# Local attention: preparation moved two units earlier, and each score issued one unit ahead

## What is computed

```python
h = shift_token(x)                       # the upper 64 channels come from the token before
q, k, v = split(h @ wqkv)                # 8 heads of 64 each
q = l2norm(q) * qs
k = l2norm(k) * ksc
q, k = rotary_xpos(q, k)                 # q * cos * scale + rotate_half(q) * sin * scale, k with 1 / scale
sim = einsum('bhwid,bhwjd->bhwij', 8.0 * q, look_around(k))
sim = where((i < j) | (i > j + WINDOW) | (j == -1), -max, sim)
o = einsum('bhwij,bhwjd->bhwid', softmax(sim), look_around(v))
x = x + o @ wo
```

## Time and profile before

| | us |
|---|---|
| median of 3 runs | 8063.11 (8062.08 to 8072.71) |
| the profiled execution | 8073.38 |
| its span, first to last instruction | 8071.7 |
| mean granted clock of TensorE | 0.813 |

### The profile page before, as it was taken

The page is one execution under the profiler, slowest core; times in us unless marked ns, Lnnn a source line. Parts: engine busy times, 40 slices in busy tenths (PEclk is TensorE's granted clock), DMA queues, the critical chain, the costliest instruction groups (busy, mean ns, idle before and its releaser), DMA issues. The chain is left out here.

```text
span 8071.7 us, 121471 instructions
## 1 busy us (share of the span) xinstructions
PE 5969.8 (74%) x45848; PEld 2884.3 (36%) x45848; DVE 4107.3 (51%) x6441; ACT 2971.3 (37%) x6472; POOL 1953.7 (24%) x1781
## 2 busy tenths in 40 slices
PE   5557567786768876666678999877777798678677
PEld 3445151114442222222234544434344333344343
DVE  4333435662427745888844444344444566444444
ACT  1002323553334541444311222345355355354453
POOL 0113032212142201444511000034143011341341
PEclk6558676887888888787785887889899888899888
DMA  1001012211121100000003221111111000110110
GB/s 44 4 30 51 14 62 68 65 49 64 48 62 43 37 16 14 0 0 0 0 7 64 52 52 44 26 41 38 31 40 38 9 1 1 47 40 15 51 39 23
DMA packets 261161, 268.98 MB, mean 33 GB/s; under 512 B 113600, under 2 KB 190656, under 8 KB 258688
## 3 DMA queue, kind: packets, MB, share of 16 engines
q1 hardware_dynamic: 250368, 240.26, 11.5%
q0 software_dynamic: 10240, 21.25, 0.8%
HBM read 122.59 MB, written 71.66 MB: 24 GB/s over the span
## 5 line engine op out<-in xcount | busy, mean ns | idle before, releaser
L2170 PE MATMUL ps<-s_l2b_hc,ident 128*128 128x512 f32 x512 | 361.4, 846 | 332.6 <-DVE s_l2b_hc L2333 332.6
L1942 DVE TENSOR_REDUCE s_l3l_negmax<-ps 128x4 f32<-128x512 f32 x256 | 175.0, 683 | 744.0 <-PE ps L1783 744.0
L2118 POOL TENSOR_TENSOR s_l2b_Bx<-s_l2b_du,s_l2b_B 128x512 f32<-128x512 f32 x256 | 406.5, 1610 | 473.3 <-ACT s_l2b_B L2240 410.4
L1873 ACT ACTIVATE s_l3l_probs<-ps,s_l3l_biases,s_l3l_q_inverse 128x128 f32<-128x128 f32 x1024 | 455.6, 462 | 55.7 <-DVE s_l3l_biases L1944 55.3
L2325 DVE TENSOR_TENSOR_SCAN s_l2b_state<-s_l2b_decay,s_l2b_Bx 128x512 f32<-128x512 f32 x256 | 389.9, 1562 | 154.6 <-ACT s_l2b_decay L2246 113.3
L1721 POOL TENSOR_TENSOR s_l3l_probs<-s_l3l_probs,s_l3l_inverse 128x512 f32<-128x512 f32 x256 | 266.9, 1043 | 830.5 <-DVE s_l3l_inverse L1923 830.3
L1745 PE MATMUL ps<-s_l3l_hs,s_l3l_wqk 128*128 128x512 f32 x512 | 305.0, 703 | 177.3 <-DVE s_l3l_prod L1897 95.5
L1057 DVE TENSOR_REDUCE s_L3a_negmax<-ps 128x1 f32<-128x128 f32 (+3 forms) x512 | 236.1, 488 | 362.0 <-PE ps L893 359.5
L638 DVE TENSOR_REDUCE s_L1a_negmax<-ps 128x1 f32<-128x512 f32 x512 | 316.5, 681 | 153.3 <-PE ps L501 152.6
L1035 ACT ACTIVATE s_L3a_pt<-ps 128x256 f32<-128x256 f32 (+3 forms) x512 | 195.3, 434 | 530.3 <-PE ps L893 528.5
L908 PE MATMUL ps<-ks,s_L3a_qs 40*128 40x256 f32 (+3 forms) x1024 | 360.2, 610 | 30.1 <-DVE s_L3a_kvsq L1072 16.5
(11 more groups left out here) (658 smaller groups left out, 13547.7 us busy)
## 6 DMA issues: line engine op xcount, KB each, us to landing
s_l3l_qk<-s_l3l_rope SPq DMA_DIRECT2D x1024, 64.0 KB
scratch_rope<-s_L3a_rope SPq DMA_DIRECT2D x32, 512.0 KB, 2.8
ks<-scratch_parts SPq DMA_DIRECT2D x384, 32.0 KB
s_L3a_qs<-scratch_rope SPq DMA_DIRECT2D x64, 128.0 KB
ks<-scratch_rope SPq DMA_DIRECT2D x64, 128.0 KB
s_L0e_slots<-scratch_sent SPq DMA_DIRECT2D x16, 396.0 KB, 5.9
s_L1e_slots<-scratch_sent SPq DMA_DIRECT2D x16, 396.0 KB, 6.3
scratch_square<-s_L1a_rows SPq DMA_DIRECT2D x24, 256.0 KB, 3.0
```

What stands on the lines that cost most here:

```text
L1873: act.activation(t["probs"][:, U % (LAG + 1), k, :], ps[:, U % 2, P * k:P * (k + 1)], ACT.Exp, bias=t["biases"][:, U % (LAG + 1), k:k + 1] ...
L2118: pool.tensor_tensor(t["Bx"][:, n % 2, k, :], t["du"][:, b % 2, k, :], t["B"][:, n % 2, :], ALU.mult).then_inc(s["bx_ready"], 1)
L2170: pe.matmul(ps[:, 4 + k, :], g["ident"][:, :], t["hc"][:, n % 2, k, :], start=(n == 0), stop=(n == STATES - 1)).then_inc(s["summed"], 1)
```

## The change

TensorE's list in a unit becomes `turns(U - 2)`, `values(U - 3)`, the output in unit 3, `scores(U + 1)`, side work. Ahead of the loop stands `scores(0)`. Preparation moves by `EARLY = 2` units: in units 0 to 5 stands what stood in units 2 to 7, and units 6 and 7 hold the first two pairs of projections of batch b+2. The lists of all engines follow (`beside` in place of `prep`). What has no unit in front of it (all of batch 0, the first two pairs of batch 1) goes into `FIRST`, ahead of the loop. The semaphore of the transfers is split into one for q's 16 and one for k's 16; a rotation waits for its own half alone. `shift` moves from unit 4 to unit 3, `shift_values` stays behind unit 7, and the four values change places.

```diff
+    EARLY = 2
+
     def prep(b, u):
-        if b == BATCH:
+        if not 0 <= b < BATCH:
             return []
         if u < 4:
             return [("proj", b, u, ab) for ab in range(2)]
         if u == 4:
-            return [("norm", b), ("v", b, 1)]
+            return [("norm", b), ("v", b, 3)]
         if u == 5:
-            return [("v", b, 0), ("v", b, 3)]
+            return [("v", b, 0), ("v", b, 1)]
...
+    def beside(b, u):
+        u += EARLY
+        return prep(b + 1 + u // UNITS, u % UNITS)
+
+    FIRST = [item for u in range(UNITS) for item in prep(0, u)] + [item for u in range(EARLY) for item in prep(1, u)]
...
-        STACKED = 16 * 32
+        STACKED = 16 * 16
...
-                sp.wait_ge(s["stacked"], START + b * STACKED)
+                sp.wait_ge(s["q_stacked"], START + b * STACKED)
+                sp.wait_ge(s["k_stacked"], START + b * STACKED)
...
-                pool.wait_ge(s["stacked"], START + b * STACKED)
+                pool.wait_ge(s["q_stacked" if e < 2 else "k_stacked"], START + b * STACKED)
...
             shift(1)
+            for e in range(EARLY):
+                rotate(1, e)
             shift_values(0)
...
-                    if u < 4 and b + 1 < BATCH:
-                        rotate(b + 1, u)
-                    if u == 4 and b + 2 < BATCH:
+                    for ahead, e in ((b + 1, u + EARLY), (b + 2, u + EARLY - UNITS)):
+                        if 0 <= e < 4 and ahead < BATCH:
+                            rotate(ahead, e)
+                    if u == 3 and b + 2 < BATCH:
                         shift(b + 2)
...
-            for u in range(UNITS):
-                for item in prep(0, u):
-                    side(item)
+            for item in FIRST:
+                side(item)
+            scores(0)
             for U in range(BATCH * UNITS + BEHIND):
                 b, u = divmod(U, UNITS)
-                if b < BATCH:
-                    scores(U)
                 if LAG <= U < BATCH * UNITS + LAG:
                     turns(U - LAG)
                 if U >= BEHIND:
                     values(U - BEHIND)
                 if b and b < BATCH and u == BEHIND:
                     side(("out", b - 1))
+                if U + 1 < BATCH * UNITS:
+                    scores(U + 1)
                 if b < BATCH:
-                    for item in prep(b + 1, u):
+                    for item in beside(b, u):
                         side(item)
```

More of the change, by code:

```diff
@@ L1612, in prep @@
         return [("qinv", b), ("v", b, 2)]
+    def beside(b, u):
+        u += EARLY
+        return prep(b + 1 + u // UNITS, u % UNITS)
+    FIRST = [item for u in range(UNITS) for item in prep(0, u)] + [item for u in range(EARLY) for item in prep(1, u)]
     def order():
-        for u in range(UNITS):
-            yield from prep(0, u)
+        yield from FIRST
         for b in range(BATCH):
@@ L1621, in order @@
                     yield ("out", b - 1)
-                yield from prep(b + 1, u)
+                yield from beside(b, u)
         yield ("out", BATCH - 1)
@@ L1673, in _ @@
                             at = 64 * r + 32 * ab
-                            sp.dma_start(t["qk"][at:at + 32, b % 2, 4 * (e // 2) + c, :], t["rope"][32 * k:32 * k + 32, e, ab, :]).then_inc(s["stacked"], 16)
+                            sp.dma_start(t["qk"][at:at + 32, b % 2, 4 * (e // 2) + c, :], t["rope"][32 * k:32 * k + 32, e, ab, :]).then_inc(s["q_stacked" if e < 2 else "k_stacked"], 16)
         @block.gpsimd
@@ L1772, in scores @@
                 if u == 0:
-                    pe.wait_ge(s["stacked"], START + (b + 1) * STACKED)
+                    pe.wait_ge(s["q_stacked"], START + (b + 1) * STACKED)
+                    pe.wait_ge(s["k_stacked"], START + (b + 1) * STACKED)
                 pe.wait_ge(s["exp_ready"], START + max(4 * (U - 1), 0))
@@ L1857, in take @@
                     taken_by(act.activation(t["v"][:, b % 2, kt, :], out, ACT.Copy), item)
-            for u in range(UNITS):
-                for item in prep(0, u):
-                    take(item)
+            for item in FIRST:
+                take(item)
             for U in range(BATCH * UNITS + LAG):
@@ L1946, in _ @@
                     invert(U - 1)
-                    for item in prep((U - 1) // UNITS + 1, (U - 1) % UNITS):
+                    for item in beside((U - 1) // UNITS, (U - 1) % UNITS):
                         if item[0] in ("proj", "norm"):
                             take(item)
-                for item in prep(b + 1, u):
+                for item in beside(b, u):
                     if item[0] in ("pick", "qinv"):
```

3 lines of the change are left out of this document (1 added, 2 removed).

## The result

The changed kernel takes **7808.25 us** (7790.88 to 7824.08, four runs) where the kernel before took 8067.91 beside it: a ratio of 0.9675 [0.965, 0.970], 260 us less. The forecast was 7740 in a range of 7665 to 7850: inside the range, 68 us above the forecast.

What follows compares the result with a forecast made beforehand. Bound by scores queued behind projections and the wait for k. Batches falling from 55.6 to 44.2 us give 273, first batches 61, starts -13: 321 us off, median 7742, written 7740, range 7665 to 7850.

Steps and rivals of the forecast that it cites:

- the maximum's wait for TensorE's order: Projection units: VectorE's maximum waits for scores queued behind projections, 5.91 us apart; 744 us idle before 256 maxima.
- the wait for k: Change of batch: first score waits for k's 16 transfers; 7.5 to 8.6 us was to shrink to about 2.7.
- maxima of projection units: Sign in VectorE's timeline: maxima 5.3 to 5.6 us apart; the forecast is wrong if they stay 5.9 apart.
- The lead: Preparation two units earlier: 11.8 us of TensorE work between first pick and next batch's first score, leaving about 2.7 wait.
- the ring above: Steps of one batch from first score through rotations, shift_values, norm, picks and k's transfers to the next: 44.2 us.
- The clock: Change of batch: the wait of 2 to 4 us for k was to pass at clock 1.00, not 0.50.
- The clock rival: Clock still falls at the change of batch: 3.8 us a batch for 28, 7845 us; chance 0.13.
- The first batches: Batch 0 of each of four calls: 36.4 us for 51.7, 61 us together.
- The start of a call: Four more projections and two rotations before the first score: at most 3.3 us more a call, 3.3 taken.
- Order does not bite: Next maximum still behind products in VectorE's queue: units stay 5.91, only the lead's 5 us comes; 7920, no separate chance.
- The lock rival: GpSimd's rotations and shift_values hold VectorE's biases, 13.6 us a batch, making 57.8; 8115 us; chance 0.04.
- TensorE alone: All handovers hidden, only TensorE's own work counts: 39 us a batch for 44.2, 7595 us; chance 0.04.

Runs made afterwards that it cites:

- e3: Changed kernel plus twelve mask products on TensorE ahead of each batch's first-score wait for q and k: 7754.23 us, 0.9616 of the kernel before.
- e1: Changed kernel with the order undone, each score again in its own unit, preparation still two units earlier: 7842.72 us, 0.9732 of the kernel before.
- e5: Changed kernel with preparation moved three units instead of two, the norm alone in its unit: 7680.36 us, 0.9528 of the kernel before.

## Why the prediction was right, and where not

**What bounded the kernel** was read rightly: the maximum's wait for TensorE's order, and the wait for k. Both shrank, from 744.0 to 162.9 us and from some 8 to some 3 us a batch. One sign did not come: maxima of projection units were to lie 5.3 to 5.6 us apart, and they follow by 3.5 and 7.7 us behind units 6 and 7, by 5.8 and 4.7 behind units 0 and 1 (medians).

**The lead.** From pick to next score I counted 11.8 us of TensorE's own work. In the ring above, picks start at 5440.27, and TensorE runs dry 2.81 us before 5454.94, at 5452.13: 11.9. The wait that is left was put at 2.7.

**The clock** is the step that failed. I took 1.00 through a wait of that length, arguing from idles of 1.12 us; a 1.12 us idle says nothing of one of 2.8. The clock at 0.50 once a batch, by which the forecast called itself wrong, came in 22 of 24 batches. The clock rival had its mechanism, and its price was too high: I took 3.8 us a batch, half of what was left of the earlier trace rows's 10.24 us, and e3 shows 1.3. This is the term that was mis-sized: with 0.7 us of small steps it makes 46.2 of 44.2, 48 us in 24 batches.

**The first batches** came to 37.5 us for 36.4, 57 of the 61 us.

**The start of a call** cost nothing where I took 3.3 us: the first maximum is at 5279.04 for 5279.36. I had set the two added units on top of the 7.27 us wait of the earlier trace rows. The timeline of the changed kernel shows both pairs in its place, just ahead of the first score at 5275:

```profile
5268.00 3.78 PE L1757 MATMUL ps<-s_l3l_hs,s_l3l_wqk 128*128 128x512 f32 x4 [0.69 <-ACT s_l3l_v L1870]
...
5272.18 2.83 PE L1757 MATMUL ps<-s_l3l_hs,s_l3l_wqk 128*128 128x512 f32 x4 [0.40 <-DVE s_l3l_prod L1909]
```

**The sum** was 321 - 48 - 4 + 13 = 282, the span's difference, so the profiled execution lies 39 us above the 7752 forecast for it. The median lies 68 above 7740: 17 more because the profiled execution is the fastest of four spread over 33 us, 10 because I had taken off what the profile of before lay above its median, and 2 of rounding. So the median lies 13 us above the band that the forecast gave itself, 7680 to 7795; it is inside the range because the range took in the clock rival's 7845.

**Order does not bite** was priced at 7920 with the lead kept. e1 shows that case at 7843: the lead alone takes 7.6 us off a batch, where I had counted 5. That the order's gain may stand or fall with the lead was in none of my rivals.

**The lock rival** fell on its size. `biases` inside a rotation, and the group of all of them (ns, min/median/max):

```profile
5417.10 0.28 DVE L1955 TENSOR_TENSOR s_l3l_biases<-s_l3l_negmax,s_l3l_q_inverse 128x4 f32<-128x4 f32 x1
...
L1955 DVE TENSOR_TENSOR s_l3l_biases<-s_l3l_negmax,s_l3l_q_inverse x256: 165/167/1372, 5279.8 to 7653.5; 128x4 f32<-128x4 f32 x128
```

I had expected up to 2.6 us, the end of both instructions of a rotation. It is held only up to the end of the first: 5417.38 falls on the border between L1707 (from 5416.09, 1.26) and L1708 (from 5417.32). Of the 256, 84 took over 0.25 us, and every one of them ended within 0.03 us of the end of a GpSimd instruction; the longest, 1.37 us, with `shift_values`' second copy. By the Trainium skill, "SBUF — State Buffer", Who interferes with whom, a VectorE instruction with two inputs in SBUF contends with a GpSimd one that reads SBUF; the trace agrees, but the hold is for one instruction of GpSimd, and in this row that was 0.1 us more than the median.

**TensorE alone** was put at 39 us a batch. e5 has TensorE busy 37.7 of its 41.7 us; that floor was not reached.

## What to carry over

A reordering and an earlier start of the same work need not be two gains that add: put the ring of one period together from rows, and ask of each edit which term of the ring it takes out. An earlier place in a queue for a consumer was worth nothing here while its producer kept its distance; give the producer its lead first. And don't judge what a wait does to the clock by idle spells that are shorter than it: filling the wait with idle products shows whether it is the wait or the clock that costs, while one more unit of lead takes away both.

## Not expected of the hardware

- Of the changed kernel's 28 waits for k, 2 to 5 us long, 24 brought the clock 0.50 in the wait or just behind it, in the ring above for 6.83 us; one of 3.25 us did not (the row and window below). e3's mask products, twelve issued and eleven on record in 2.76 us, kept 1.00 in the wait's place.

```profile
5828.44 0.38 PE L1789 MATMUL ps<-s_l3l_bandb,s_l3l_identb 128*128 128x512 bf16 x1 [3.25 <-issue]
...
5825.00:5874.59 49.59, 40.21 (x453) 24.21 (x453) 29.69 (x54) 30.65 (x96) 25.39 (x22) 1.00 0.21 50
```

- VectorE's floor over 128x512 (L1912), one input in SBUF, took 0.40 us in 27 of 32 cases in the kernel before, where GpSimd's scaling started 0.2 us after it, and 1.47 to 1.53 in all 32 of the changed one, where a rotation of GpSimd had started ahead of it (ns, min/median/max; before, then changed). The output projection hides it.

```profile
L1900 DVE TENSOR_SCALAR s_l3l_rows<-s_l3l_rows x32: 395/395/1530, 5257.0 to 7889.9; 128x512 f32<-128x512 f32 x32
```

```profile
L1912 DVE TENSOR_SCALAR s_l3l_rows<-s_l3l_rows x32: 1473/1482/1526, 5254.2 to 7602.0; 128x512 f32<-128x512 f32 x32
```
